# Gating thirteen of sixteen sequences inside the first attention of a four-layer network

## The reference

```python
# layer 0: rope attention (16 heads of 8), then experts
x = layernorm(x + attention0(x))
logits = x @ gate_w + gate_b                   # 8 experts
scores = softmax(logits); topk_s, topk_i = top_k(scores, 2)
for i in range(8):
    wi = score of expert i where it is among the two, else 0
    h = relu(x * wi @ w1[i] + b1[i]);  y = h @ w2[i] + b2[i]
    out = where(wi > 0, y, out)                # the last chosen expert wins
x = layernorm(x + out)
# layer 1: attention over a 32-wide normed latent, then a channel mix
# layer 2: sigmoid attention, then experts;  layer 3: linear attention, MLP
```

## Time and profile before

| what | value |
|---|---|
| median of 2 runs | 1764.41 us (1764.37 to 1764.45) |
| the profiled execution: its time, its span | 1759.57 us, 1757.8 us |
| PE busy | 1465.9 us, 83% of the span |
| DVE busy | 1014.1 us, 58% |
| ACT busy | 725.2 us, 41% |
| POOL busy | 242.0 us, 14% |
| the chain that ended last | PE 71%, DVE 10%, issue 7%, POOL 5%, ACT 4%, DMA 2% |

### The profile page before, as it was taken

The page is one execution under the profiler, slowest core; times in us unless marked ns, Lnnn a source line. Parts: engine busy times, 40 slices in busy tenths (PEclk is TensorE's granted clock), DMA queues, the critical chain, the costliest instruction groups (busy, mean ns, idle before and its releaser), DMA issues.

```text
span 1757.8 us, 33649 instructions
## 1 busy us (share of the span) xinstructions
PE 1465.9 (83%) x12538; PEld 1102.7 (63%) x12538; DVE 1014.1 (58%) x2788; ACT 725.2 (41%) x1282; POOL 242.0 (14%) x466
## 2 busy tenths in 40 slices
PE   5999999996069229999999996499998899998977
PEld 3666666655069215666666654366665799997667
DVE  4677776762346335566666655824443566665856
ACT  0444444432146122443444333356766455553322
POOL 0000000000521540010101101200000000001423
PEclk9999999985589656899999897779999899999989
DMA  9100000000022100000000000000000000000001
GB/s 314 50 1 1 1 1 1 2 1 1 36 66 69 48 17 1 1 1 1 1 1 1 1 1 1 1 2 1 2 1 1 1 2 2 1 2 1 1 16 34
DMA packets 32689, 30.39 MB, mean 17 GB/s; under 512 B 4544, under 2 KB 29328, under 8 KB 31888
## 3 DMA queue, kind: packets, MB, share of 16 engines
q1 hardware_dynamic: 30480, 24.05, 4.3%
q0 software_dynamic: 2048, 4.20, 0.8%
HBM read 18.01 MB, written 10.22 MB: 16 GB/s over the span
## 4 chain that ended last, share of the span: by engine, by line
PE 71%; DVE 10%; issue 7%; POOL 5%; ACT 4%; DMA 2%; SPq 0%; POOLq 0%; DVEq 0%; ACTq 0%
PE S L337 12%; PE O L1534 7%; PE O L407 6%; PE S L323 5%; PE A L311 4%; PE S L326 4%; PE A L292 4%; ACT probs L628 3%; PE A L312 3%; PE O L411 3%; PE S L1516 2%; PE A L428 2%; PE O L1945 2%; PE O L365 2%; PE S L1517 2%
## 5 line engine op out<-in xcount | busy, mean ns | idle before, releaser
L628 ACT ACTIVATE probs<-S 128x1024 f32<-128x1024 f32 x288 | 289.9, 1025 | 188.3 <-PE S L337 180.4
L800 DVE TENSOR_REDUCE nm<-S 128x4 f32<-128x1024 f32 x128 | 151.7, 1214 | 91.8 <-PE S L337 91.6
L155 POOL TENSOR_TENSOR ve<-mv,eps 128x2 f32<-128x2 f32 x112 | 26.6, 237 | 1083.5 <-DVE mv L147 1083.5
L1602 ACT ACTIVATE probs<-S,eb 128x256 f32<-128x256 f32 x256 | 107.5, 473 | 117.3 <-PE S L1518 117.3
L1534 PE MATMUL O<-ew,probs 128*128 128x128 f32 x1024 | 138.1, 278 | 0.4 <-ACT probs L1602 0.2
L635 ACT COPY OT<-O 128x512 f32<-128x512 f32 x96 | 56.2, 586 | 190.4 <-PE O L411 190.4
L407 PE MATMUL O<-probs,V 128*32 128x256 f32 x1536 | 128.0, 407 | 4.7 <-ACT probs L628 3.4
L1534 PEld LDWEIGHTS O<-ew,probs 128*128 128x128 f32 x1024 | 125.2, 192 | 5.3 <-ACT probs L1602 3.6
L311 PE MATMUL A<-hi,spread 128*128 128x256 f32 x384 | 111.9, 322 | 19.8 <-DVE lo L779 8.8
L166 DVE TENSOR_SCALAR X<-res,mv,rstd 128x128 f32<-128x128 f32 x224 | 85.5, 423 | 67.2 <-POOL rstd L159 66.4
L337 PEld LDWEIGHTS S<-QM,KS 32*128 32x128 f32 x1024 | 78.1, 201 | 61.4 <-issue 61.4
(11 more groups left out here) (332 smaller groups left out, 3141.6 us busy)
## 6 DMA issues: line engine op xcount, KB each, us to landing
ew<-in_w SPq DMA_DIRECT2D x2, 2048.0 KB
moe_rows<-zeros SPq DMA_DIRECT2D x1, 2944.0 KB, 12.7
xin<-moe_rows SPq DMA_DIRECT2D x23, 128.0 KB, 2.3
ew<-in_w SPq DMA_DIRECT2D x2, 1024.0 KB
out<-X SPq DMA_DIRECT2D x16, 128.0 KB, 1.8
moe_made<-ctx_sb SPq DMA_DIRECT2D x12, 128.0 KB, 1.8
moe_made<-ctxT SPq DMA_DIRECT2D x11, 128.0 KB, 1.8
probs<-in_spread SPq DMA_DIRECT2D x1, 1024.0 KB, 5.0
```

The costliest lines, as they stand in the source:

```text
L628: act.activation(c.probs[:, n].rearrange("p b g l -> p b (g l)"), c.S[:, n % 2], ACT.Exp if soft else ACT.Tanh, scale=self.scale).then_inc ...
L800: dve.tensor_reduce(c.nm[:, 1, 2 * pr:2 * pr + 2, 2 * u:2 * u + 2], slot.rearrange("p b (g k) -> p b g k", g=2), AX.X, ALU.max, negate=Tru ...
L1602: act.activation(w["h"][:, x % 2, j], c.S[:, x % 2, bank, col:col + L], ACT.Relu, bias=w["b1"][:, x * self.NJ + j:x * self.NJ + j + 1]).th ...
```

## The change

- Sequences 0 to 12 are gated inside the first attention. With the transposes of sequence s (3 to 15), PE also transposes the finished `X` of sequence s-3 into the second half of the same bank, ACT copies 512 columns in place of 256 (`xT2`), PE makes the logits ahead of the value products (`pe_logits`), and DVE adds the gate bias behind its value copy (`add_bias`). PE waits for that `X`, and ahead of its second query/key product for the bias sum.
- Sequences 13 to 15 are gated in the expert phase as before, each waiting for its own `X`.
- The small products that fold a scale and shift into layer 1's weights (`fold_products`, `fold`) move from the phase's start to the middle of routing. The two routing products on PE now wait for `wt` too. One PSUM result is first copied to SBUF (`early`). ACT makes all 32 blocks of `z`.
- `scales` is done for one sequence at a time, and each gather from the fifth sequence on is issued behind one of them. `FIRST = 16`: all sums and norms stay in the expert phase, so that the hooks in the second attention (`pool_behind`, `dve_behind`, `act_behind`) issue nothing. The gather buffers are no longer a part of `OT`.
- The second attention is entered when the last tile is summed, and PE's transposes wait for `X` by sequence. In `latent_step` the second query product moves ahead of `latent_T`.
- Layer 2's expert weights share memory with layer 0's, so their loads (two of 1 MB and some small ones) move from the start of the program to behind the last tile's store.

```diff
@@ Attention
         def x_transposes(s, par):
+            if self.before:
+                rows = self.before.e["x"]
+                pe.wait_ge(rows.sem, rows.at(s))
             for t in range(T):
                 mm = pe.transpose(c.A[:, 0, t * P:(t + 1) * P], c.X[:, s, t, :], c.ident[:])
+            if self.gated(s):
+                pe.wait_ge(e["x"].sem, e["x"].at(s - 3))
+                for t in range(T):
+                    mm = pe.transpose(c.A[:, 0, L + t * P:L + (t + 1) * P], c.X[:, s - 3, t, :], c.ident[:])
             mm.then_inc(e["xt_ps"].sem, 1)
@@ values
+            if self.gated(s):
+                self.after.pe_logits(pe, s - 3)
@@ projections
                 pe.wait_ge(e["v"].sem, e["v"].at(s))
+                if self.gated(s):
+                    pe.wait_ge(self.after.s["lgc"], s - 2)
@@ latent_step
                 projections(k + 1, 0, (0,))
+                projections(k + 1, 1, (0,))
                 latent_T(k + 1, nxt)
-                projections(k + 1, 1, (0,))
@@ act x_copy
-            act.copy(c.xT[:], c.A[:, 0, 0:L]).then_inc(e["xt"].sem, 1)
+            cols = 2 * L if self.gated(s) else L
+            act.copy(c.xT2[:, 0:cols], c.A[:, 0, 0:cols]).then_inc(e["xt"].sem, 1)
@@ dve v_copy
+            if self.gated(s):
+                self.after.add_bias(dve, s - 3, self.after.logits_place(s - 3))
@@ Routed
+    ALONE = 13
+    def pe_logits(self, pe, q):
+        w = self.w
+        if q == 0:
+            pe.wait_ge(*self.loaded)
+        out = self.logits_place(q)
+        for t in range(T):
+            mm = pe.matmul(out[:, t * NE:(t + 1) * NE], self.c.xT2[:, L + t * P:L + (t + 1) * P], w["gate"][:], start=True, stop=True)
+        return mm
+    def add_bias(self, dve, q, out):
+        if q == 0:
+            dve.wait_ge(*self.loaded)
+        return dve.tensor_tensor(self.w["LG"][:, T * q:T * q + T, :], out.rearrange("p (t x) -> p t x", x=NE),
+                                 self.w["bg"][:].unsqueeze(1).broadcast_to((P, T, NE)), ALU.add).then_inc(self.s["lgc"], 1)
+    FIRST = 16
@@ Routed.pool
-        for g in range(4):
-            for q in range(4 * g + 4, min(4 * g + 8, B)):
-                gather(q)
-            scales(g)
+        for q in range(self.FIRST):
+            self.scales(pool, q)
+            if q + 4 < B and q + 4 <= self.FIRST:
+                self.gather(pool, q + 4)
@@ enter
-            else:
+            elif n == 2:
+                eng.wait_ge(experts0.s["yg"], experts0.NT)
+            elif n > 2:
                 eng.wait_ge(phases[n - 1][1].e["x"].sem, phases[n - 1][1].e["x"].at(done))
@@ sync
+            sp.wait_ge(experts0.s["y_ps"], experts0.NT)
+            sp.wait_ge(experts0.s["bias"], 2 * experts0.NT)
+            for dst, src in loads["moe2"]:
+                sp.dma_start(dst, src).then_inc(loaded["moe2"], 16)
```

More of the change, by code:

```diff
@@ L191, in __init__, with gated @@
         self.e = c.events(**ev)
-        self.rest = None
+        self.rest = self.after = self.before = None
         self.v_bank = c.O[:, 0] if kind == "latent" else c.A[:, 1]
         self.scale = HD ** -0.5 if kind != "sigmoid" else 2 * HD ** -0.5
+    def gated(self, s):
+        return self.after is not None and s >= 3
     def pool(self, pool):
@@ L692, in latent_step @@
             o_copy(k, 1)
+            if self.before:
+                self.before.act_behind(act, k)
         def sigmoid_step(k, par, has_tail, has_front):
@@ L1791, with __init__ @@
     SLOTS = 256
-    def __init__(self, c, name, layer, w):
-        self.c, self.layer, self.w = c, layer, w
-        self.K = 1 if layer == 0 else 2
+    ALONE = 13
+    def __init__(self, c, name, w, before):
+        self.c, self.w, self.before = c, w, before
         self.hidden = w["hidden"]
@@ new lines, in written, with pool_behind @@
+    def written(self, act, q):
+        c, w, e = self.c, self.w, self.e
+        act.wait_ge(e["nmr"].sem, e["nmr"].at(q))
+        for t in range(T):
+            n = T * q + t
+            act.activation(c.X[:, q, t, :], c.X[:, q, t, :], ACT.Identity, bias=w["nmr"][:, n:n + 1],
+                           scale=w["rstds"][:, n:n + 1]).then_inc(e["x"].sem, 1)
+    FIRST = 16
+    def pool_behind(self, pool, k):
+        q = self.FIRST + k
+        if q + 1 < B:
+            self.gather(pool, q + 1)
+        if q < B:
+            self.scales(pool, q)
@@ L1947, in output @@
             mm.then_inc(s["y_ps"], 1)
+        for q in range(self.ALONE, B):
+            transposes(q)
+            if q > self.ALONE:
+                logits(q - 1)
+        logits(B - 1)
+        self.fold_products(pe)
+        pe.wait_ge(s["gate"], self.WEIGHT)
+        pe.matmul(c.O[:, 0, 0:B * T * NE], w["earlier"][:], w["ohb"][:], start=True, stop=True)
+        pe.matmul(c.O[:, 1, 0:B * T * NE], w["ones_b"][:], w["ohb"][:], start=True, stop=True).then_inc(s["rank_ps"], 1)
         tile_transposes(0)
@@ L1997, in relu @@
             act.copy(w["w2c"][:, par, 0:NJ * P], w["w2x"][:, x, :]).then_inc(s["w2c"], 1)
+        act.wait_ge(s["gate"], self.DIFF)
+        act.activation(w["EX"], w["LG"], ACT.Exp).then_inc(s["ex"], 1)
+        act.wait_ge(s["gate"], self.WEIGHT)
+        for n in range(B * T):
+            act.activation(w["z"][:, n // T, n % T, :], c.X[:, n // T, n % T, :], ACT.Copy, scale=w["wt"][:, n:n + 1])\
+               .then_inc(s["z"], 1)
         act.wait_ge(s["gate"], self.TILES)
@@ L2006, in act @@
             relu(j)
[L2007 to L2012 removed]
+        for q in range(self.FIRST):
+            self.written(act, q)
     def dve(self, dve):
         c, s, w, e, NJ, NA = self.c, self.s, self.w, self.e, self.NJ, self.NA
[L2016 removed]
```

436 lines of the change are left out of this document (222 added, 214 removed).

## The result

The changed kernel takes 1797.68 us (median of 2 runs, 1794.98 and 1800.38) against 1764.41: a ratio of 1.0194, 95% interval 1.0145 to 1.0243, or +33.3 us. The forecast was 1766.5, the range 1757 to 1775, so the time lies 23 above the range.

What follows compares the result with a forecast made beforehand. PE was taken to bound the attention, a short dependent chain gating and routing, POOL gather and norm. +8.2 - 19.3 + 1.0 + 11.3 + 0.9 = +2.1 gave 1766.5 on the runs' median; range 1757 to 1775.

Steps and rivals of the forecast that it cites:

- The second attention: Query product ahead of the latent's transposes: maxima still wait for `latT`, nothing gained in a normal step, steps of 23.70.
- +0.9 for the first step: Second attention's first step, at half clock: PE is late and the moved product delays the transposes, +0.9 once.
- signs of being wrong: POOL waiting for DVE's statistics at the first `scales`, steps over 23.3, or second attention steps of 23.2.
- The rival on the clock: More PE idling before the second attention puts five more steps at the low clock: +37.8, 1804; chance 0.02.
- Attention, +8.2: First attention: added transposes and narrow products take PE 0.63 in each of 13 steps, +8.2.
- Gating and routing, -18.3: After the first attention: first wide reduction 19.3 earlier; routing +1.0 for waits on `wt`, the fold and an extra copy.
- Scatter and tiles, 0: Scatter and the 23 tiles: same work in the same order, so no change.
- Gather and norm, +11.3: POOL's narrow `scales`, 1.66 each, give +14.5; the shorter end gives -2.4, ACT's earlier first copy -0.8.
- the moved loads: Rival: layer 2's loads delay the first gathers' rows, POOL waits about 5 once, 1771.5; chance 0.13.
- DVE stayed ahead of PE at the maxima: Rival: DVE or ACT becomes last in 13 first-attention steps, +2.6 to +5.2, about 1770.5; chance 0.13.
- The query product filled no wait: Rival: the moved product fills PE's wait in 15 second-attention steps, -8.2, 1758; chance 0.10.
- The second attention didn't start early: Rival: it starts behind the first norm, hiding most of gather and norm's 55 us: 1715; chance 0.01.

Runs made afterwards that it cites:

- e2_order_alone: The kernel before with only the second attention's second query product moved ahead of the latent's transposes: 1799.31 us, ratio 1.0212 to before.
- e1_order_back: The changed kernel with the second attention's second query product back behind the latent's transposes: 1757.62 us, ratio 0.9960 to before.
- e7: The changed kernel with the second query product issued a second time, ahead of the latent's transposes: 1748.69 us, ratio 0.9921 to before.
- e9: The changed kernel with the second query product issued a second time, right behind the maxima: 1766.29 us, ratio 1.0021 to before.

## Why the prediction was wrong, point by point

- **The second attention: the step that failed.** "They start no earlier, so nothing is gained in a normal step", and steps of 23.70. The first half is right: an undisturbed step is 23.7 in both, and the 0.54 wait moved. What the step left out is that PE's clock depends on what lies around that wait. It measured +43.1, of which 39.7 lie in the 13 steps, with 8 more long ones; e2_order_alone shows that the swap alone does it. The +0.9 for the first step did not come either (the first two steps took 56.1, before 56.3). None of the signs of being wrong that the prediction lists came up; it named none for a longer step. The rows for it were there: 3 of 13 steps of before were already 28.0 long, so the clock already fell inside this phase, and the step at the low level stood in the earlier trace rows, but I used it for the rival alone.
- **The rival on the clock** had the size (1804) and the wrong cause, idle time ahead of the phase. In e1_order_back that idle time is still there, and the loss isn't. Its reason against, "it has nothing more to fall", looked only at the head of the phase. The price per step, 7.55, came from a cold step at the head; a long step here costs 4.3 to 5.7.
- **Attention, +8.2, measured -0.7.** The mechanism is right, the size off: 0.59 on PE against 0.63, and only 0.46 in the step's length, with 0.08 in the first of the 13 steps, so +5.5. The other 6.2 go the other way, and that the total came out at nothing is luck. One step of before was long by 2.65 (25.05 in place of 22.40, from 283.9) and none of after. The third `xT` copy comes 0.9 earlier (58.9, 59.9). In the tail, where PE now gates the last sequences, the stretch from 403 to 411 has the clock at 0.64 with PE busy 5.40, in place of 0.50 with 3.30, which goes with 2.7 less. These are readings of one execution each: over all profiles the last `X` write ends at 407.5 to 410.6 in the three kernels with the old attention, and at 409.9 to 418.8 in the eleven with the changed one.
- **Gating and routing, -18.3, measured -18.7.** Held: -19.3 up to the first wide reduction, as forecast, and +0.6 behind it for the forecast +1.0.
- **Scatter and tiles, 0, measured +1.2.** Held.
- **Gather and norm, +11.3, measured +7.9.** POOL's list does set it. The narrow scales cost 3.88 - 2 x 1.25 = 1.38 a sequence in place of 1.66, since the next gather follows the last product sooner than behind a wide one: 12 x 1.38 - 2 x 2.70 = +11.2, less 2.4 and 0.8 gives 8.0. That is the lower bound of this term (1.4 each, +8); the 1.66 a sequence was mis-sized.
- **The other rivals.** With the moved loads the first sum came later, 7.1 behind the first gather in place of 3.9. The text said that the first 5 us cost nothing, and POOL didn't wait. The Trainium skill's rule ("DMA: Bandwidth & Descriptors", section "Queues, rings and completion order"), that an engine takes turns between queues, agrees with this delay, though no run isolates it, and it stayed hidden. DVE stayed ahead of PE at the maxima, though by 0.05 and not by 0.15. The query product filled no wait. The second attention didn't start early.
- **The sum and the range.** Without the second attention's 43.1 and the rest's 2.7 the profile would have been 10.4 ahead. That is 1754.0 on the median, below the range; e1_order_back, which is the changed kernel without the swap, took 1757.62, just inside its edge, and 8.8 (0.4 to 13.8) less than the kernel before beside it. The terms ahead of the second attention sum to +1.2, so they were too high together as well: by 2.7 in the attention and 3.4 in the gather and norm, and for the rest by what differs between two executions. The range had no term for the number of long steps, at 4.3 to 5.7 us each, nor for the scatter of one kernel between executions (1744.59 to 1765.40 in the ten of e1_order_back). How much of that scatter long steps make is not shown; the head of the first attention has a part, since its third `xT` copy comes between 58.9 and 64.4 over the profiles.

## What to carry to other kernels

Before moving work on PE within a step, count the steps of the profile that are already long at a low granted clock; if there are some, the order around PE's waits can be worth more than the waits themselves, and a swap that leaves every duration alone can cost 2%. Where PE waits in an otherwise full step, test a repeated matmul in or ahead of the wait: 0.6 us of useless work a step brought 48 us back in the changed kernel. In the kernel before, where few steps were long, the same gave nothing that these runs resolve. And make a change in its parts: of this one, the gating inside the attention gave 18.7 for 5.5 on PE, the seam did nothing until sums were moved over it (15 more), the narrow scales cost 8 to 9, and one incidental swap of two lines cost some 40 and hid the rest.

## What the hardware showed that I had not expected

- PE's clock fell out of a step in which PE is busy for 22.2 of 23.7 us, shortly behind a wait of 0.54. The step's other pauses on PE are one of 0.35 for `ctx_sb` and two of 0.2, which no run varied. The swap takes the 0.35 and the 0.54 further apart, from 2.1 to 3.0 us, but they are 3.2 apart in e7 too, with 2 long steps, so the distance is not the cause. In the slow stretch PE is busy without a pause, and it still takes 13.7 or 10.2 us before the clock is back (719.3 to 732.9 and 750.0 to 760.2 in after).
- The Trainium skill ("TensorE: Matmul & The Clock Gate", section "A second HAM failure mode: psum-queue depth-cycling") tells of a kernel in which frequent small pauses between groups of matmuls made the clock swing. The runs here agree that pauses far shorter than the step are enough, and add how fine it is: 11 long steps of 13 with the product 0.9 us ahead of where it gives 2 or 3, at the same sum of pauses.
- A step has discrete lengths: 23.7, 28.0 and 29.5 after, 24.2 and 27.0 in e9. The length lost goes with how long the clock stays low: in after the four steps of 29.5 hold a low stretch of 13.7 each and the seven of 28.0 one of 10.2, and in e9 the six of 27.0 one of 6.8.
- What stays open is which step falls. Steps with the same wait and the same busy time in the 2 us around it (1.34) differ in it, and two waits (8 long steps) did no worse than one (9 and 11). No run here tells this.
